# A two-layer attention and mixture-of-experts kernel on one core: other ways to norm, a folded projection, an item table computed later

## The reference, cut to what matters

```python
x = x + _L0_conv_ref(_ln_c(x), ...)     # 1x1 qkv, 5x5 depthwise + grouped 1x1, linear attention, projection, batch norm
t = _to_tokens(x)
t = t + _L0_ffn_ref(_ln_t(t), ...)      # mixture of 8 experts, top 2, gelu, biases
x = _from_tokens(t, x)
x = x + _L1_conv_ref(_ln_c(x), ...)     # softmax attention per image
t = _to_tokens(x)
t = t + _L1_ffn_ref(_ln_t(t), ...)      # mixture of 16 experts, top 2, silu gate

def _ln_c(v, eps=1e-06):                # over the 128 channels of a token
    m = jnp.mean(v, axis=1, keepdims=True)
    s = jnp.var(v, axis=1, keepdims=True)
    return (v - m) / jnp.sqrt(s + eps)

# inside _L1_conv_ref, n = m = 256 tokens of an image
scores = jnp.einsum('bcn,bcm->bnm', q, k) / jnp.sqrt(c)
attn = jax.nn.softmax(scores, axis=-1)
out = jnp.einsum('bcm,bnm->bcn', v, attn)
return _conv1x1(out, wo, bo)            # v = wv x + bv, so the projection wo follows wv
```

## Time and profile before

| what | value |
|---|---|
| median of 3 runs | 446.56 us (446.3 to 446.96) |
| the profiled execution's own time | 447.75 us |
| its span (first to last instruction) | 446.0 us |
| around the span | 1.75 us |
| mean granted TensorE clock | 0.892 of full |
| busy: PE, DVE, ACT, POOL | 352.9, 222.9, 210.9, 178.0 us |

### The profile page before, as it was taken

One profiled execution on the slowest core, in us unless ns is written; L12 is line 12 of the kernel. 1 busy time (PEld: TensorE's weight loads), 2 busy tenths in 40 slices (PEclk: granted clock), 3 DMA queues, 4 the chain that ended last, 5 costly groups with the idle time before them and its releaser, 6 DMA issues.

```text
span 446.0 us, 7931 instructions
## 1 busy us (share of the span) xinstructions
PE 352.9 (79%) x2404; PEld 301.4 (68%) x2404; DVE 222.9 (50%) x565; ACT 210.9 (47%) x554; POOL 178.0 (40%) x202
## 2 busy tenths in 40 slices
PE   3889999997956598957999399898267988977813
PEld 1359999985734598957998265776246888877802
DVE  3618555513675156534776373776841343444306
ACT  4651333333574256734663364566533565554304
POOL 3819554400033655573556000003066555555530
PEclk9999999999896679995999789999665999999875
DMA  7444444324822546310111700000311111111146
GB/s 239 202 74 99 102 96 83 48 37 70 343 73 88 194 176 239 124 49 30 37 38 43 194 2 0 1 1 0 96 42 41 43 43 37 44 36 37 35 119 194
DMA packets 34184, 38.47 MB, mean 86 GB/s; under 512 B 3680, under 2 KB 28640, under 8 KB 33376
## 3 DMA queue, kind: packets, MB, share of 16 engines
q1 hardware_dynamic: 22620, 25.79, 19.8%
q0 software_dynamic: 4096, 8.40, 6.0%
q10 hardware_dynamic: 7428, 3.77, 3.9%
HBM read 24.31 MB, written 7.34 MB: 71 GB/s over the span
## 4 chain that ended last, share of the span: by engine, by line
PE 63%; DMA 8%; DVE 8%; ACT 6%; issue 6%; another core or an unknown queue 5%; ACTq 1%; POOL 1%; SPq 1%; POOLq 0%; DVEq 0%
PE bank L1342 18%; PE bank L1359 12%; PE bank L1252 10%; DMA ln_sq<-y 2%; PE bank L1204 2%; PE bank L1351 2%; PE bank L1424 2%; PE bank L1269 2%; PE bank L1189 2%; ACT w_block L684 2%; PE bank L1383 2%; POOL y L517 1%; PE bank L1133 1%; DMA x_rows<-tok,token 1%
## 5 line engine op out<-in xcount | busy, mean ns | idle before, releaser
L1342 PE MATMUL bank<-x_cols,w_block 128*128 x688 | 104.0, 300 | 20.5 <-ACT w_block L684 9.7
L1342 PEld LDWEIGHTS bank<-x_cols,w_block 128*128 128x128 f32 x688 | 94.1, 212 | 24.5 <-issue 24.3
L510 POOL DMA_INDIRECT x_rows<-tok,token x64 | 60.6, 947 | 65.2 <-DVE dest L970 26.9
L517 POOL DMA_INDIRECT y<-wide,dest x64 | 62.1, 970 | 49.4 <-DVE wide L1046 39.6
L1359 PE MATMUL bank<-w_down,h_cols 128*128 x500 | 75.4, 290 | 4.8 <-DVE wide L1046 3.2
L1359 PEld LDWEIGHTS bank<-w_down,h_cols 128*128 128x128 f32 x500 | 66.9, 203 | 7.3 <-issue 7.0
L1252 PE MATMUL bank<-cmap,cw 128*128 128x112 f32 (+2 forms) x480 | 57.4, 275 | 1.9 <-DMA cmap<-heads 1.9
L1252 PEld LDWEIGHTS bank<-cmap,cw 128*128 128x128 f32 x480 | 55.7, 192 | 3.7 <-DMA cmap<-heads 2.7
L684 ACT ACTIVATE w_block<-w_up 128x512 f32 x86 | 53.6, 623 | 0.9 <-issue 0.9
L321 POOL TENSOR_TENSOR cw<-taps 128x640 f32<-128x640 f32 x24 | 35.7, 1514 | 36.7 <-PE bank L1252 29.5
L1029 DVE TENSOR_TENSOR h_cols<-h_in,bank 128x256 f32<-128x256 f32 x47 | 19.8, 421 | 53.4 <-ACT h_in L701 32.0
(11 more groups left out here) (188 smaller groups left out, 524.8 us busy)
## 6 DMA issues: line engine op xcount, KB each, us to landing
w_up<-in_up_dram SPq DMA_DIRECT2D x4, 1024.0 KB
cmap<-heads SPq DMA_DIRECT2D x48, 64.0 KB
w_up<-in_w_dram SPq DMA_DIRECT2D x1, 2048.0 KB, 7.7
w_down<-in_w_dram SPq DMA_DIRECT2D x1, 2048.0 KB, 13.7
tok<-ln_sq SPq DMA_DIRECT2D x8, 256.0 KB, 2.4
w_down<-in_down_dram SPq DMA_DIRECT2D x4, 512.0 KB
wide<-y SPq DMA_DIRECT2D x8, 256.0 KB, 5.6
ln_sq<-y ACTq DMA_DIRECT2D x8, 256.0 KB, 6.1
```

Source lines behind the costliest of these rows:

```text
L510: pool.indirect_dma_start(out=x_rows[:, j % RING, :], out_offset=None, in_=tok_dram[r], in_offset=bass.IndirectOffsetOnAxis(ap=token[r][:, ...
L517: pool.indirect_dma_start(out=y_dram[r], in_=y_acc[:, s * C:(s + 1) * C], in_offset=None, out_offset=bass.IndirectOffsetOnAxis(ap=dest[r][ ...
L1342: mm = pe.matmul(bank[2 + j % UPS][:, i * 128:(i + 1) * 128], w_block[:, j % 3, i * 128:(i + 1) * 128], x_cols[:, bass.ds(place[j] & ((NB ...
```

## The change

- **First norm.** `x_tok` and its loads are gone. PE turns each tile of x itself (`turn_x`), after six fp16 filler matmuls of 512 columns (`fill`); DVE takes the statistics from PSUM. The four columns of 1/std of a chunk are turned by PE into four rows (`turn_inverse`), ACT copies these into four partitions of `inv_row`, which is zero elsewhere, and four matmuls with the selector `row_of` spread them. Two fillers stand ahead of `turn_inverse` and two behind it, in each chunk.
- **Around it.** q's four heads are all made inside the conv loop, at steps 2 to 5. Unit 0's four maps have a semaphore each (`map_first`), and PE waits for one at a time. DVE's relu of q moves from step 4 to step 8. `late_w` is loaded behind all taps.
- **Second norm.** x is turned again after the expert sum (`turn_new`), statistics come from PSUM, and the stages of a chunk follow one another in one loop on DVE, with `ln_root_of` on ACT woven between the weighings. Centring moves into wq, wk, wv (PE at step 10, DVE copies at step 11). q and k of chunk 0 wait for three scaled chunks, those of the others for four.
- **Projection.** wo times wv is made once (step 12), so the attention of an image gives its projected sum; `sq_o`, L1092 and L1440 are gone, and `xs` is updated by image. The banks of the second `token_rows` change.
- **Item table.** It is computed ahead of the wait for `rt_inverse`, so `token` and `dest` are written after it; PE now waits for the items alone.

```diff
@@ sync @@
-            xt_load(0)
-            xt_load(1)
-            x_load(0)
...
+            for c in range(NCH):
                 sp.dma_start(chunk(xs, c), chunk(x, c)).then_inc(x_in[c], 16)
...
-                            .then_inc(map_in[n], 16)
+                            .then_inc(map_in[n] if n else map_first[g], 16)
@@ scalar @@
                     act.activation(ln_r[:, 0, tiles], x_mv[:, tiles, 1], ACT.Sqrt, bias=eps[:, 0:1]).then_inc(x_root, 1)
-                    act.wait_ge(x_inv, c + 1)
                     if c >= 2:
                         act.wait_ge(x_spread, c - 1)
-                    for i in range(4):
-                        act.activation(ln_diag[:, c % 2, i, :], ident[:, :], ACT.Copy,
-                                       scale=ln_r[:, 1, 4 * c + i:4 * c + i + 1]).then_inc(x_diag, 1)
+                    act.wait_ge(x_inv_turned, c + 1)
+                    act.activation(inv_row[0:4, c % 2, :], bank[7][0:4, 0:128], ACT.Copy).then_inc(x_inv_row, 1)
...
+            def ln_root_of(c):
+
+                act.wait_ge(ln_aggr, 4 * c + 4)
+                act.activation(ln_r[:, 0, 4 * c:4 * c + 4], x_mv[:, 4 * c:4 * c + 4, 1], ACT.Sqrt, bias=eps[:, 0:1])\
+                    .then_inc(ln_root, 1)
...
                     act.activation(xc[:, i * 128:(i + 1) * 128], xc[:, i * 128:(i + 1) * 128], ACT.Copy,
                                    scale=pair_w[:, 0, i:i + 1]).then_inc(y_weighed, 1)
+                    if behind and i % 4 == 3 and i > 3:
+                        behind(i // 4 - 1)
@@ vector @@
-                dve.wait_ge(rt_inverse, r + 1)
-                s = totals[:, 0:NB]
-                step(dve.tensor_copy(place_of[:, :], s))
...
+
+                dve.wait_ge(rt_inverse, r + 1)
+                step(dve.tensor_copy(place_of[:, :], totals[:, 0:NB]))
...
+            for c in range(NCH + 3):
+                if c < NCH:
+                    moe_sum(0, c)
+                if 1 <= c <= NCH:
+                    moe_add(0, c - 1)
+                if c >= 3:
+                    ln_scale(c - 3)
+                if 2 <= c < NCH + 2:
+                    ln_diagonals(c - 2)
+                if 1 <= c <= NCH:
+                    ln_stats_of(c - 1)
@@ tensor @@
+            def spread_scale(c):
+                pe.wait_ge(x_inv_row, c + 1)
+                for j in range(4):
+                    mm = pe.matmul(bank[4 + c % 3][:, j * 128:(j + 1) * 128], row_of[:, j, :], inv_row[:, c % 2, :],
+                                   start=True, stop=True)
+                mm.then_inc(x_spread, 1)
...
+            pe.wait_ge(rows_of, 4)
+            fill(4, 6)
+            turn_x(0)
+            turn_x(1)
+            turn_x(2)
...
+                fill(4 + c % 3, 2)
+                turn_inverse(c)
+                fill(4 + c % 3, 2)
                 spread_scale(c)
                 if c >= 1:
                     head(0, c - 1)
...
             def queries_keys(c):
+                pe.wait_ge(ln_out, (3, 4, 4, 4)[c])
+                pe.wait_ge(ln_aggr, TT)
...
+            y_turn = y_columns(0)
+            for c in range(NCH + 2):
+                if c < NCH:
+                    y_turn(c)
+                if 1 <= c <= NCH:
+                    turn_new(c - 1)
+                if c >= 2:
+                    ln_spread_of(c - 2)
+            for c in range(NCH):
+                queries_keys(c)
```

More of the change, by code:

```diff
@@ L253, in metaformer @@
         kv_ones = sem("kv_ones")
+        map_first = [sem(f"map_first{i}") for i in range(GU)]
         map_in = [sem(f"map_in{u}") for u in range(len(UNITS))]
@@ L702, in moe_act, with weigh_first @@
                                 .then_inc(m.act, 1)
-            def weigh_first(r):
+            def weigh_first(r, behind=None):
                 y_load(act, r, 1)
@@ new lines, in moe_add, with ln_stats_of @@
+            def moe_add(r, c):
+                dve.wait_ge(y_turned, NCH * r + c + 1)
+                dve.tensor_tensor(chunk(xs, c), chunk(xs, c), bank[c][:, :], ALU.add).then_inc(x_moe, 1)
+            def ln_stats_of(c):
+                dve.wait_ge(ln_turned, c + 1)
+                for i in range(4 * c, 4 * c + 4):
+                    dve.bn_stats(x_stat[:, i, :], bank[c][:, (i % 4) * 128:(i % 4 + 1) * 128]).then_inc(ln_stats, 1)
+                for i in range(4 * c, 4 * c + 4):
+                    dve.wait_ge(ln_stats, i + 1)
+                    dve.bn_aggr(x_mv[:, i, :], x_stat[:, i, :]).then_inc(ln_aggr, 1)
@@ L1072, in _ @@
                                 bank[V_BANKS[g]][:, :].rearrange("p (j q) -> p j q", j=4)).then_inc(sq_v_out, 1)
-            for i in range(B + 6):
+            for i in range(B + 3):
                 if i < B:
@@ L1090, in _ @@
                     k = i - 3
+                    image = xs[:, k * S:(k + 1) * S]
                     dve.wait_ge(sq_mm, k + 1)
-                    dve.tensor_scalar(sq_o[:, k, :], bank[4 + k % 2][:, 0:S], vec("bv"), None, ALU.add)\
-                        .then_inc(sq_out, 1)
-                if i >= 7 and i % 2 == 1:
-                    c = (i - 7) // 2
-                    dve.wait_ge(wo_mm, c + 1)
-                    dve.scalar_tensor_tensor(out=chunk(xs, c), in0=bank[WO_BANKS[c]][:, :], scalar=vec("bo"),
-                                             in1=chunk(xs, c), op0=ALU.add, op1=ALU.add).then_inc(x3_ready, 1)
+                    dve.scalar_tensor_tensor(out=image, in0=bank[4 + k % 2][:, 0:S], scalar=bvo[:, :], in1=image,
+                                             op0=ALU.add, op1=ALU.add).then_inc(x3_ready, 1)
             router(1, E1)
             moe_vector(1, E1, NI1, w_up1)
-            moe_sum(1)
+            dve.wait_ge(rt_weights, 2)
+            for c in range(NCH + 1):
+                if c < NCH:
+                    moe_sum(1, c)
+                if c >= 1:
+                    moe_add(1, c - 1)
         @block.tensor
@@ L1426, in weigh_v @@
                 mm.then_inc(sq_mm, 1)
-            for i in range(B + 5):
+            for i in range(B + 3):
                 if i < B:
@@ L1481, in _laid_out @@
     return {
[L1482 removed]
+        "x_c": x_c, "qkv": qkv, "taps": taps.reshape(128, NG, TAP), "late": late,
         "w1": w1.transpose(1, 0, 2).reshape(C, E0 * F0),
```

261 lines of the change are left out of this document (125 added, 136 removed).

## The result

The changed kernel takes **451.94 us** in the median (450.03 to 453.73, 7 runs); the kernel before, run beside it, takes 446.56 (445.1 to 449.47, 7 runs). The ratio is 1.0103, with a 95% interval of 1.0068 to 1.0137: slower by about 1%. The forecast was 449.1, range 443.0 to 452.5. The profiled execution took 453.44 us, its span 451.7, 5.7 us more than the span of before.

A forecast was written before the change was run, and what follows sets the result against it. PE's list was taken to set the time (63% of the chain). Terms +1.3 + 0 + 5.5 - 3.8 - 1.0 = +2.0, plus 0.5 for clock skew, on 447.75, less 1.19, gave 449.1 us; range 443.0 to 452.5.

The forecast's parts named there:

- rival of the low clock: Both norms: the clock stays low, first norm +3.2, second +7.0, sum +5.4, so 452.0 us; chance 0.12.
- First norm, +1.3: First norm: the last k head copy ends at 22.5 instead of 21.23 us, +1.3; bounds -3 to +3.2.
- the ring: First norm: short waits between DVE, ACT and PE; DVE starts 2.8 us late at its head, last scale at 19.7.
- bound of a clock low until 12 us: First norm: upper bound of its term, +3.2 us if PE's clock is low until 12 us.
- Map semaphores and q heads, 0: Map loads and conv loop: PE may start 2.4 us sooner, but this is eaten there; 0, bounds -0.7 and +0.5.
- Second norm, +5.5 with bounds 0 and +7: Second norm: ring waits and eight q and k matmuls behind the last spread delay the scores, +5.5 us.
- choice of 286 in the range of the clock: Second norm: scores start at 286 us, taken between 283.4 (full clock throughout) and 287.6 (clock rising after q begins).
- Attention, -3.8: Attention: four projections of 0.86 us go, 24.4 us from scores to the rows' end; -3.8, bounds -2.5 and -4.5.
- Item table, -1.0: Both routings: items ready earlier, place_of and gather later, -0.5 in the second; -1.0 for both, bounds -2.5 and +1.
- Queries not late, 443.5: Second norm: DVE's loop packs, scores start at 281 us, sum -3.1, so 443.5 us; chance 0.30.
- Stalls, +-1.5 us: Whole kernel: stalls with no known releaser, some 20 us, may shift with big loads; 1.5 us allowed either way.

The follow-up runs named there:

- nofill: Changed kernel without the four fillers a chunk in the first norm, the six at the start kept; 453.17 us, one run.
- lean: Changed kernel without per-chunk first-norm fillers, with q and k between the second norm's spreads and ACT's roots one weighing later; ratio 0.9946 to the kernel before.
- both_old: Changed kernel with both norms of before; folded projection and centring, item table, map semaphores and q heads in the loop stay; ratio 0.9915 to the kernel before.
- norm1_old: Changed kernel with the first norm of before (x_tok loaded, statistics from SBUF, no fillers); ratio 1.0084 to the kernel before.
- warm2: Changed kernel with 18 fp16 filler matmuls of 512 columns on PE in the second norm; 450.12 us, one run.
- qk_between: Changed kernel with q and k of a chunk made as soon as it is scaled, between the second norm's spreads; ratio 1.0066 to the kernel before.
- fold_only: Kernel before with only the attention's folded projection and centring; both norms and item table stay; ratio 0.9865 to the kernel before.
- root_later: Changed kernel with ACT's root of a chunk one weighing later in the second norm; 451.24 us, one run.
- norm2_old: Changed kernel with the second norm of before, q and k behind each chunk's scaling; ratio 1.0017 to the kernel before.
- mix: Changed kernel with the first norm of before, q and k between the second norm's spreads and ACT's roots one weighing later; ratio 0.9881 to the kernel before.

## Why the prediction was right in its direction, and what it sized wrongly

The forecast was slower at 449.1 for the reason named, the second norm; the measured 451.94 is 2.8 us more, and lies in the range close to the rival of the low clock (452.0).

- **First norm, +1.3.** Mis-sized. Fillers (2.72 for six, taken 2.6), turns and statistics were near: 7.28 for the first statistics, taken 7.7. But the ring that follows was longer: last scaling at 20.54, taken 19.7, maps at +2.3, the loop's end at +1.8. Part of that is this one profile: over five kernels with this first norm the last scaling comes at 19.52 to 20.54, and the means are +1.7 and +1.6, close to the forecast. It was thought that ACT's order holds the last chunk; nofill and lean show that the fillers ahead of and behind each turn are all of the cost, 1.6 us: without them the last scaling comes at 18.23 and 18.83, with the first norm of before at 18.10 to 18.87. The bound of a clock low until 12 us did not come: from 11.27 us on a chunk's spread takes 1.16, as it does to the end. The granted clock can't be used for this stretch. It reads 1.00 there in every profile, also where the durations are those of the lower level: the first six fillers at 0.45 each against 0.59 for two later on, and the four spread records of before in 3.50.
- **Map semaphores and q heads, 0.** Right: both_old starts the loop 2.6 us earlier and ends it 0.5 earlier. In the changed kernel the first matmul was expected at 25.5 to 26.5 and came at 26.82, with the later maps.
- **Second norm, +5.5 with bounds 0 and +7.** The mechanism was right in each of its lines (gaps of 0.66 on DVE around sums 2 and 3, weighings released by statistics, q and k in one block), and the size was wrong: +8.1, beyond the bound (+6.8 in norm1_old and nofill, inside it). Set 0.8 later, as the weighing was, the forecast has the diagonals' end at 274.5 and the scores at 286.8; measured are 275.16 and 289.40. So 0.7 comes from the ring, 0.1 from the last spread, and 1.85 from q, k and v, which took 12.32 where 10.47 were reckoned at the full clock. In norm1_old, with 35.89, the diagonals end when the forecast has them, to 0.2 us, and the 1.0 too much in q, k and v (11.48) is nearly all of the miss. The mis-sized term is the choice of 286 in the range of the clock: it took the row of before, 0.83 from 258 us on the earlier trace rows, for a stretch in which PE was no longer busy throughout. Counted at the low clock (286.8 to 287.6 by the prediction) the term would have been 6.3 to 7.1. The Trainium skill, TensorE: Matmul & The Clock Gate, Part 4 (PE-mode transpose), says that a transpose doesn't count as busy for the clock as a matmul does. This trace agrees in the main, with 0.50 to 0.67 over 23 us of turns and spreads, and with warm2's 1.00 from 268 us on once fp16 matmuls were put between them. What no run separates is whether the turns or the idle time between them kept it low: qk_between and warm2 filled both.
- **Attention, -3.8.** -3.3 (-3.4 in fold_only); 24.9 us to the end of the rows, where 24.4 was forecast.
- **Item table, -1.0.** -0.39 in the second routing and -0.45 in the first, each a little less than the 0.5 that the forecast had derived for it.
- **Low clock in both norms, 452.0.** It gives the time, but not the way: in the first norm PE had its full speed from the first spread on, in the second it was low. Its +3.2 was really +1.8. (The -1.05 between the loop's end and the first inverse belongs to no edit: from 111 to 114 us PE ran at 1.00 and before at 0.53. both_old, lean, warm2 and root_later had the short stage too, with 29.83 to 29.94, norm2_old, mix and nofill not, with 30.71 to 30.78.)
- **Queries not late, 443.5.** Refuted, but it is what the repaired kernels do (norm 2 at 28.1).
- **Stalls, +-1.5 us.** Too little: up to 2.5 us in one stage between executions of one kernel.

The sum by measured stages is +1.8 -1.05 +8.13 -3.27 -0.84 (both tables) +0.9 (experts and rest) = +5.7; forecast +2.5. The 2.6 of the second norm is most of the miss. That the median came within 0.1 us of the low-clock rival is chance: its two norms were reckoned at +10.2 and cost +10.0, but with the first too dear and the second too cheap, and the -1.05 and the experts' +0.9 nearly cancel.

## What to carry to other kernels

When a chunk's work is rearranged so that its last consumers stand in one block behind the last producer, count it twice: the block no longer fills the gaps between the producers, and an engine with gaps may drop to the lower clock just when the block comes. Put the consumers between the producers, one chunk behind, and give an in-order helper engine (ACT's roots) a chunk of slack before its next independent work. Fillers are tested one by one: the same fp16 matmuls gave 3.6 to 5.0 us in the second norm and cost 1.6 in the first, where PE ran as fast without them. Read a stage from more than one profile before an edit is priced: the same second norm took 35.9 and 37.2 us. Of a change of several parts, time the simplest one alone: here no other kernel gained more.

## What the runs showed of the hardware

In the expert stages the engines stop for some microseconds with no releaser that the profile knows. In experts 1 PE's two longest idle times come at the same two places in all 13 profiles, whatever was edited: at 154 to 158 us and at 197 to 204 us, 2.7 to 5.2 us each. The timeline of the changed kernel at the first, with the other engines' idle times, and PE's at the second; then PE's of fold_only at both:

```profile
157.28 0.28 ACT L683 ACTIVATE x_cols<-bank 128x128 f32<-128x128 f32 x1 [6.04 <-remote]
157.43 0.69 DVE L1002 TENSOR_TENSOR h_in<-bank,wT 128x512 f32<-128x512 f32 x1 [7.38 <-remote]
...
157.70 0.30 PE L1398 MATMUL bank<-ident,x_rows 128*128 128x128 f32 x1 [4.91 <-ACT x_cols L683]
...
200.12 1.22 PE L1389 MATMUL bank<-x_cols,w_block 128*128 x4 [3.58 <-ACT w_block L680]
```

```profile
156.94 0.30 PE L1358 MATMUL bank<-ident,x_rows 128*128 128x128 f32 x1 [2.68 <-ACT x_cols L687]
...
200.38 1.00 PE L1349 MATMUL bank<-x_cols,w_block 128*128 x3 [4.90 <-issue]
```

The two of the changed kernel are 8.5 us of its span. Their cause was not tried.

An fp16 matmul of 512 columns took 0.45 us at the lower clock (3.62 for eight in warm2); at the full clock, in the same kernel, two took 0.59 and four 1.03, so each further one 0.22. An f32 one takes 0.86 to 0.88 there (two records; 7.03 for eight matmuls in warm2). `bn_stats` on a 128 by 128 tile took the same 0.22 us from PSUM as from SBUF.
